# Moving the expert chunks of a two-layer pipeline into other slots, and ScalarE's bank copies ahead of its exponential

## The reference

```
q  = einsum('bnd,dhk->bnhk', x, Wq)                       # 16 heads of 64
qf = (exp(q_dash - diag - max) + 1e-6) / 8                # q_dash = q * dn @ proj.T, 64 features
attn = (qf @ kv) / (qf @ sum_kf)                          # per head
out1 = layernorm(x + attn @ Wo)
h    = elu(out1 @ W1 + b1);  enc = layernorm(out1 + h @ W2 + b2)
x    = x + gate_a * enc
# mixture of experts on h = layernorm(x) * (1 + c) + s: 16 experts of width 64, two per token
shared = (silu(h @ sfc1.T) * (h @ sfc2.T)) @ sfc3.T       # width 256
moe    = sum_e dispatch[t, e] * (silu(h @ w1[e].T) @ w2[e].T)
x      = x + gate_b * (moe + shared)
```

## Time and profile before

| what | us |
|---|---|
| time, median of 3 runs (range) | 3342.69 (3342.19 to 3344.24) |
| the profiled execution's own time | 3342.81 |
| its span, first to last instruction | 3341.0 |
| one step of the loop, square to square | 73.85 |
| TensorE, VectorE, ScalarE, GpSimd busy over the span | 83%, 78%, 71%, 30% |
| TensorE, VectorE, ScalarE busy in that step | 66.80, 48.27, 62.93 |

### The profile page before, as it was taken

How to read it: one execution, slowest core, us unless ns; L and a number is a source line. 1 busy time by engine, 2 the same in 40 slices (tenths; PEclk the granted TensorE clock), 3 DMA queues, 4 the chain that set the end, 5 groups by cost and what they waited for, 6 DMA issues and landing times. The chain is left out here.

```text
span 3341.0 us, 53375 instructions
## 1 busy us (share of the span) xinstructions
PE 2778.6 (83%) x15818; PEld 2085.7 (62%) x15818; DVE 2613.5 (78%) x4414; ACT 2362.5 (71%) x5178; POOL 1014.7 (30%) x687
## 2 busy tenths in 40 slices
PE   2367988888888888888888897689999889999986
PEld 1044664665665565566566575577887777778875
DVE  2999999999999999999999952566666666666663
ACT  2556676686676777668667654468888888888873
POOL 0544444444344344444434310011111111111111
PEclk6578999999999999999999999899999999999998
DMA  2000000000000000000000001000000000000000
GB/s 111 8 4 12 22 4 20 17 3 20 17 3 20 17 17 6 20 17 3 20 17 0 18 18 67 26 15 18 28 17 17 22 20 17 17 17 28 17 9 15
DMA packets 49779, 64.41 MB, mean 19 GB/s; under 512 B 3584, under 2 KB 36416, under 8 KB 49184
## 3 DMA queue, kind: packets, MB, share of 16 engines
q1 hardware_dynamic: 47392, 54.93, 5.1%
q10 hardware_dynamic: 2304, 8.46, 0.6%
HBM read 41.78 MB, written 21.60 MB: 19 GB/s over the span
## 5 line engine op out<-in xcount | busy, mean ns | idle before, releaser
L797 POOL TENSOR_TENSOR acc<-acc,shared 128x1024 f32<-128x1024 f32 x256 | 610.7, 2386 | 878.9 <-DVE shared L1122 811.9
L1122 DVE TENSOR_TENSOR_SCAN shared<-shared 128x1024 f32<-128x1024 f32 x256 | 600.1, 2344 | 14.4 <-issue 4.9
L942 PEld LDWEIGHTS bank<-one_sb,hid 128*128 128x128 f32 x4096 | 478.4, 192 | 30.4 <-issue 17.2
L942 PE MATMUL bank<-one_sb,hid 128*128 128x128 f32 x4096 | 481.3, 275 | 14.6 <-ACT hid L662 14.6
L163 POOL TENSOR_SCALAR n_ve<-n_mv 128x4 f32<-128x4 f32 x96 | 57.8, 602 | 1163.8 <-DVE n_mv L141 1163.8
L890 PE MATMUL bank<-S,pick_sb 96*128 96x512 bf16 x512 | 209.6, 415 | 235.1 <-DVE shared L1134 120.9
L630 ACT ACTIVATE shared<-shared,aneg 128x512 f32<-128x512 f32 (+1 forms) x512 | 341.3, 723 | 61.9 <-DVE shared L1122 46.2
L1134 DVE TENSOR_TENSOR shared<-shared,bank 128x1024 f32<-128x1024 f32 x256 | 312.5, 1221 | 15.0 <-POOL acc L797 4.6
L890 PEld LDWEIGHTS bank<-S,pick_sb 96*128 96x128 bf16 x512 | 50.4, 99 | 430.6 <-DVE shared L1134 184.4
L1115 DVE TENSOR_TENSOR shared<-shared,bank 128x1024 f32<-128x1024 f32 x256 | 309.4, 1209 | 0.4 <-PE bank L890 0.3
L662 ACT ACTIVATE hid<-banks,one_sb 128x512 f32<-128x512 f32 x304 | 208.1, 690 | 110.4 <-PE bank L942 70.3
(11 more groups left out here) (274 smaller groups left out, 7044.9 us busy)
## 6 DMA issues: line engine op xcount, KB each, us to landing
kv_dram<-Gs ACTq DMA_DIRECT2D x16, 516.5 KB, 3.1
kvl<-kv_dram SPq DMA_DIRECT2D x16, 516.5 KB, 3.5
xs<-in_x SPq DMA_DIRECT2D x16, 256.0 KB, 2.9
x<-in_x SPq DMA_DIRECT2D x16, 256.0 KB, 3.0
x_dram<-x SPq DMA_DIRECT2D x16, 256.0 KB, 2.1
h_dram<-hT SPq DMA_DIRECT2D x16, 256.0 KB, 2.0
h<-h_dram SPq DMA_DIRECT2D x16, 256.0 KB, 2.7
x2s<-x_dram SPq DMA_DIRECT2D x16, 256.0 KB, 2.6
```

The lines of the kernel that those rows point to most:

```text
L797: pool.tensor_tensor(acc[:, :, :], acc[:, :, :], zz[:, k % 2, :, :], ALU.add)\
L942: last = pe.matmul(bank1(f"down{e}")[:, j * D:(j + 1) * D], hid[:, e % 2, f, j * P:(j + 1) * P], w2[:, e, f, :], start=(f == 0), stop=(f = ...
L1122: dve.tensor_tensor_scan(h[:, :, :].rearrange("p g t -> p (g t)"), dec[:, k % 2, :, :].rearrange("p g t -> p (g t)"), u[:, :, :].rearrange ...
```

## The change

It moves chunks 1 to 9 to other slots. Slots 2 and 3, in which ScalarE has its two elu, get none. Slots 8 and 9 get two each. `XR` lists the second chunk of a slot. `DOWN` follows. In slots 2, 3, 4 and 6 (`EXP_LATE`) ScalarE's exponential comes behind the copies qT and aT. In slots 4 and 6 (`EXP_FIRST`) the chunk's Silu comes behind the exponential, and VectorE's product behind elu and the quotient.

```diff
-        XQ = {q + 1: q for q in range(NX)}
-        DOWN = {6: (0,), 7: (1, 2), 8: (3,), 9: (4, 5), 10: (6,), 11: (7,)}
+        XQ = {1: 0, 4: 1, 5: 2, 6: 3, 7: 4, 8: 5, 9: 7, 10: 9}
+        XR = {8: 6, 9: 8}
+        EXP_FIRST = (4, 6)
+        EXP_LATE = (2, 3, 4, 6)
+        DOWN = {6: (0,), 7: (1,), 8: (2, 3), 9: (4,), 10: (5, 6), 11: (7,)}
...
+            if slot in XR:
+                q = XR[slot]
+                orderD += [(f"x{q}", MOE, sl_ok, q + 1), (f"y{q}", MOE, hm_ok, q + 1)]
...
-                        if e is not None and slot in XQ:
+                        if e is not None and slot in XQ and slot not in EXP_FIRST:
                             silu(XQ[slot], e)
-                        if c is not None and slot < M:
+                        if c is not None and slot < M and slot not in EXP_LATE:
                             feature(slot, c)
...
+                        if c is not None and slot in EXP_LATE:
+                            feature(slot, c)
+                        if e is not None and slot in EXP_FIRST:
+                            silu(XQ[slot], e)
+                        if e is not None and slot in XR:
+                            silu(XR[slot], e)
...
                         if c is not None and at_slot(slot, 3) is not None:
                             turn_quotient(at_slot(slot, 3), c, s)
+                        if e is not None and slot in XR:
+                            hidden(XR[slot], e, s)
+                            factor(XR[slot], e, s)
...
-                        if e is not None and slot in XQ:
+                        if e is not None and slot in XQ and slot not in EXP_FIRST:
                             chunk(XQ[slot], e)
...
                             quotient(at_slot(slot, 2), c)
+                        if e is not None and slot in EXP_FIRST:
+                            chunk(XQ[slot], e)
+                        if e is not None and slot in XR:
+                            chunk(XR[slot], e)
```

## The result

The changed kernel takes 3375.95 us (median of 4 runs, 3371.84 to 3376.57) against 3342.44 for the kernel before on the same chips: ratio 1.0097, 95% interval 1.0085 to 1.0110. It is 34 us slower. The forecast was 3386, slower with a chance of 0.77.

What follows compares the result with a forecast made beforehand. TensorE, busy for 66.80 of a 73.85 us step, was taken as the bound, with ScalarE's relief hidden. Terms -0.33 + 0.03 + 0.15 + 3.35 = +3.2 us over 14 steps, tail -2, gave 3386 us, range 3335 to 3406.

Steps and rivals of the forecast that it cites:

- Slots 2 and 3: Slot 2 gains 0.33 us, slot 3 nothing on TensorE's path: -0.33 us a step, bounds -0.93 and 0.
- Slots 4 and 5: The removed load was hidden, chunk 1's y replaces a TensorE wait: +0.03 us a step, bounds -1.28 and +1.0.
- Slots 6 and 7: New order forms a chain up to slot 8's `output`, though one `down` leaves: +0.15 us, bounds -0.9 and +1.5.
- Slots 8 to 11: Full TensorE gets more x, y, `down` and two bank waits, loses a 0.83 us wait: +3.35, bounds +1.2 and +4.2.
- The step: One loop step with attention, feed-forward and experts grows by +3.2 us to 77.05 us, in 14 steps.
- The edges: Outside steps 2 to 15: tail -2 us, between -5 and +3; no term for steps 0 and 1.
- The range: Whole kernel's time: 3363 to 3402 us for the likeliest case, 3335 to 3406 us for 8 times in 10.
- The clock: Slots 2 and 3: as thin as step 1's, which ran at 1.00, so no fall to 1.2 GHz was priced.
- the forecast's own sign: Slots 2 and 3: a granted clock under 1.00 there would make the clock the cause instead.
- A: Slots 2, 3, 5 and 7: freed ScalarE sets the pace, faster, -1.5 x 14 = -21, 3322 us; chance 0.16.
- B: Slots 4 to 7 shrink by about 2.5 us, gain equals what is added: 3343 us; chance 0.07.
- D: Slots 4 and 6: late order costs 1.0 and 1.5 us more a step, +35 on top, 3421 us; chance 0.12.

Runs made afterwards that it cites:

- places alone: Changed kernel with its new chunk slots, but exponential, copies and Silu in the old order in every slot: 3381.08 us, ratio 1.0118.
- one chunk: Kernel before with only one chunk moved, none in slot 3 and two in slot 8, orders as before: 3369.37 us, ratio 1.0080.
- no loads: Chunks' Silu replaced by a Copy that needs no table, in the kernel before: 3306.33 us (0.9895), and in the changed kernel: 3343.41 us (1.0006).
- `down` into the waits: Changed kernel with one `down` moved ahead of the turned norm in slot 8 and of the logits in slot 9: 3364.56 us, ratio 1.0067.
- the order alone: Changed kernel's order on ScalarE and VectorE, with chunks and `down` in their old slots: 3346.34 us, ratio 1.0012.

## Why the prediction was right, point by point

*Slots 2 and 3:* right, -0.33 as forecast. The step without chunks was the measure of what the loads there could be worth, and the new slots took its 8.13 and 8.35.

*Slots 4 and 5:* right in mechanism. The load ahead of the Silu was hidden, the wait took its place (0.37 became 1.24). Slot 5 is 6.32 us from q to q in both traces. The term was +0.03 and is -0.23, all of it in slot 4. I had set the y of chunk 1, 0.5 us, against the 0.45 that the trace shows as idle before elu's product. The y costs 0.48, but without the wait the stretch is shorter by 0.70. A wait costs more than its idle time: the bank waits show 0.45 and cost 0.62, the wait for aT shows 0.83 and costs 0.94.

*Slots 6 and 7:* right in size, +0.15 against +0.23. The sum hides its parts: one `down` has left, and three waits have come, 0.29 and 0.34 us for VectorE's exponent and 0.17 for aT.

*Slots 8 to 11:* right, +3.35 against +3.19, with the bank waits at 1.62 and 1.63 us from x to the next user of the bank and without the wait of 0.83, which was worth 0.94: 1.62 + 1.63 + 0.89 - 0.94 = 3.20. The term came from rows of the tail and of other slots. It was tested from four sides: places alone, one chunk, no loads, and `down` into the waits.

*The step:* forecast 77.05, measured 76.72 and, with the clock, 76.84. Over 12 loop steps the difference to the forecast is 2.5 us of the 10 by which the time was missed.

*The edges:* this is where most of the miss lies. I took +3.2 us for 14 steps and -2 for the tail, and 0 for steps 0 and 1. Those two gained 1.66 us (112.10 against 113.76), because with no chunk to hold it the copy ahead of the exponential uses ScalarE's wait for VectorE. The order is what gains there, since the new places alone leave the two steps at 113.68. Step 2 rose by 2.72. From step 15 on, the intervals between the starts of GpSimd's last operation of each batch (ob) were 71.69, 56.54 and 24.25 us and are 73.32, 51.71 and 24.21: the first rose by 1.6 instead of 3.2, the second fell by 4.8 where I had -2 for the whole tail. The mechanism there was named and sized too small. From the second to the third elu of step 16 it was 5.56 us and is 1.82, with the wait of 1.74 gone. Two runs part the 4.8: the new places alone have 51.43, so the order has no share in it; and between the two kernels without loads the interval falls only from 47.93 to 45.78, so 2.2 us of it need no load and some 2.7 hang on the loads.

*The range:* 3363 to 3402 for the likeliest case does not follow from the bounds as they stand. Half of their distances, added plainly, are -2.56 and +1.75 us a step and -1.5 and +2.5 for the tail, 3349 to 3413. The measured time lies in both.

*The clock:* this step failed. I priced no fall, because step 1 has the same pauses at a clock of 1.00. The same pause of 1.53 us stands in steps with and without a fall, so one clean step was no proof. It cost little, 1.7 us of the 34, and the forecast's own sign, that a clock under 1.00 would make the clock the cause, was too strong: steps at a clock of 1.00 take 76.72 us. The Trainium skill, "TensorE: Matmul & The Clock Gate", section "Why this matters for your kernels", warns of idle gaps between bursts of matmuls. In kind two runs agree with it (0.80 after the pause of slot 2, 0.81 after that of slot 3 once it was 2.26 us long). But the gaps that it warns of are longer than each of these pauses, so by its letter it did not speak against this change, unlike what the prediction says, and the traces go beyond it. What decides in which step the clock falls stays open.

*The rivals:* A fell with the two kernels without loads, B with the measured time, D with the order alone and the places alone. D's count for the late order was far too high, and in the new places even its sign was wrong.

*Luck:* the +3.2 of a step was right for the reasons given. But the 1.7 us of the clock, which I had not priced, made up for a part of what the edges missed; without it the forecast would have been 12 us off instead of 10.

## What to carry to other kernels

Before work is moved to take load off an engine, replace the suspected cost by something free and time that: 23 us of table loads a step were worth 2.1 here. Do it for each stage: in the tail the same loads counted for more. In a stretch where one engine is full, each piece that is moved there costs its full length on that engine (here 1.01 us for x and y), and if its bank is wanted next, also the turn-around to the reader (here 0.62 us); put a piece that needs no bank behind it. And a wait that is removed usually uncovers the next one, so price the second before counting the first.

## What the runs showed that was not expected

The clock fell from 2.4 to 1.2 GHz for a part of a slot after pauses of 1.53 us, in every second step of the changed kernel, with the same instructions and the same pause each time, and in every third, every fourth or no step of other versions with that pause. With a pause of 2.26 us a fall cost 0.6 to 1.1 us a slot, and once 2.7 (11.09 against 8.34). A step without any of 18 table loads was only 2.1 us shorter. And the new order alone, which costs 0.6 us a step where chunks are in their old slots, was worth some 1.4 us in step 0, where there are none.
